# One loop for all rounds in a graph layer: two column groups per step, checks in the middle, a bias product ahead of the last sums

## The chip, the cores and the metric

The kernel runs on one core of a Trainium2 chip. The metric is the device time of one execution in microseconds, the median of several runs. The profile is of one further execution. The span that it shows runs from the first instruction to the last; the time of that execution is a little longer.

## What is computed

Edges carry 128 features each and are sorted by the node `dst` that they point to. Their features are summed per node; node features, sums and one constant row go through a small network, and the result is added to the node features and normalised.

```
agg = segment_sum(edge_attr, dst, num_segments=6250)      # 200000 x 128 -> 6250 x 128
h   = relu(concat([x, agg, u[0]], axis=1) @ W1 + b1)      # 6250 x 128
y   = x + h @ W2 + b2
out = (y - mean(y)) / sqrt(var(y) + 1e-5)                 # per row
```

All is float32. The edge features are 102 MB, by far the largest input; x and the output are 3.2 MB each.

## The kernel before

**Steps and rounds.** 199,680 edges are cut into 65 steps of 3,072 edges (1.5 MB); 320 edges are left as a rest. Steps run from the highest nodes down to node 0; the code counts them with `t`, 0 to 64. Five steps make a round (`lap`, 0 to 12). `dst` follows a square law, so a step near the top spans up to 195 nodes and a step near node 0 only a few. Each round finishes one block of 512 nodes (`BLOCK`), except that the last one leaves only nodes 0 to 127 for the end.

**One step.** VectorE (DVE) makes a one-hot matrix of each run of edges (`hot`, line 580) and one for the rows of partial sums (`row_hot`, line 596). TensorE (PE) does `level1` (line 808): 48 matmuls on 64x32 tiles of its array, each a pair of instructions in the profile, which sum edges into 128 rows of partial sums in PSUM, `rows_ps`. ScalarE (ACT) copies these to SBUF (line 416). PE does `level2` (line 820): two full matmuls that add the rows onto columns, one column per node, in `cols_ps`; DVE adds them to `agg_t` at the step's base column (`add`, line 606), and the next `level2` waits for that addition. The one-hots are made three steps ahead (`AHEAD`).

**Two kinds of rounds.** Rounds 0 to 5 (`sparse_lap`) use 224 columns and put `level2` of step t-1 behind `level1` of step t; `rows_ps` has three buffers. Rounds 6 to 12 (`dense_lap`) use 128 columns and put `level2` of step t right behind `level1` of step t. PE and DVE have a loop for each kind.

**A block of 512 nodes.** x is loaded (ACT's DMA queue), transposed on PE (line 828), copied by ACT (line 436); two products make the hidden layer (line 834 with x, line 843 with `agg_t`); ACT applies relu (line 447); PE multiplies by W2 (line 852); DVE adds (line 618), takes statistics (628, 634, 637) and normalises (643). GpSimd (POOL) adds b2 to x (`bias_add`, line 371) and raises to the power -0.5 (line 380). These pieces stand between the steps of the following round.

**Loads and stores.** SyncE (SP) issues the edge loads into five slots; the load of step t+5 waits for the end of `level1` of step t. The stores of finished blocks stand on SP's queue behind all 65 loads; the last one (line 316) waits for the last normalisation.

```
for t in range(SLOTS, steps):
    sp.wait_ge(level1_done, t - SLOTS + 1)
    load(t)
for i in range(final):
    store(i)
```

**Checks.** The kernel assumes bounds on the nodes that a step reaches. `judge` (DVE, lines 648 to 663) checks them in round 11, PE sums the counts in round 12 (lines 908 to 910) and `make_plan` writes the flag `plan`; were it 0, a slow general path would do all again.

**Filler products.** In the last round PE multiplies `iota` by `ident` into unused columns ahead of steps 62, 63 and 64 (line 901). Nothing reads the result.

## Time and profile before

| what | value |
|---|---|
| median of 3 runs | 281.1 us |
| lowest and highest run | 280.07 and 281.37 us |
| the profiled execution, own time | 281.48 us |
| its span | 279.8 us |
| PE, weight loads (PEld), DVE, ACT, POOL busy | 77%, 60%, 60%, 18%, 15% of the span |
| moved by DMA | 110.06 MB, mean 393 GB/s |
| mean granted clock of TensorE | 0.954 |

The time outside the span is 281.48 - 279.8, some 1.7 us. A busy share is an average over the whole span and says nothing of what a stage waits for. The chain of work that ended last puts 62% on PE and 17% on "issue", time in which the engine waited for nothing that the profile shows; the arrival of a load in SBUF is often such a wait.

### The profile page before, as it was taken

The numbers are of one execution on the slowest core, as the hardware profiler recorded it, in microseconds if no ns is written. First come the engines' busy times: TensorE is split into PE (matmuls) and PEld (weight loads), VectorE is DVE, ScalarE is ACT, GpSimd is POOL, SyncE is SP. The second block draws the span as 40 slices with busy tenths as digits, with TensorE's granted clock in tenths as the row PEclk, the third lists the DMA queues.
The fourth block names the chain that finished last, engine by engine and source line by source line (L and its number), as shares of the span: only waits on it lengthen the run. The fifth ranks groups of instructions, "written<-read, shape, count | busy, mean of one in ns | idle before, by whom it ended". The sixth has DMA issues, their size and how long they took to land.

```text
span 279.8 us, 15302 instructions
## 1 busy us (share of the span) xinstructions
PE 214.5 (77%) x6767; PEld 169.0 (60%) x6767; DVE 167.7 (60%) x425; ACT 51.3 (18%) x100; POOL 40.8 (15%) x49
## 2 busy tenths in 40 slices
PE   0988599986786696696867499898867867767982
PEld 0866487755665575575545378677655655655761
DVE  7932375774665655754854426958565563797552
ACT  0511031311220220221200211322221121120210
POOL 6400020220300400400401100303020030021020
PEclk9986899999999999999997869999999999997998
DMA  7999999999999999999999999999999999999991
GB/s 249 351 387 399 401 399 401 401 400 401 402 399 403 401 400 402 401 401 412 417 411 414 414 401 406 418 417 418 413 418 415 418 416 414 411 418 413 413 396 62
DMA packets 30623, 110.06 MB, mean 393 GB/s; under 512 B 1976, under 2 KB 3150, under 8 KB 30606
## 3 DMA queue, kind: packets, MB, share of 16 engines
q1 hardware_dynamic: 27508, 105.83, 95.3%
q10 hardware_dynamic: 3098, 4.00, 4.1%
q8 instruction: 10, 0.16, 0.2%
q14 instruction: 7, 0.06, 0.1%
HBM read 106.63 MB, written 3.20 MB: 393 GB/s over the span
## 4 chain that ended last, share of the span: by engine, by line
PE 62%; issue 17%; DMA 13%; DVE 5%; POOL 1%; ACT 1%; DVEq 0%; POOLq 0%; ACTq 0%
PE rows_ps L808 33%; PE cols_ps L820 15%; DMA slots<-in_edge_attr 13%; PE hid_ps L852 4%; PE hid_ps L834 3%; PE hid_ps L843 2%; PE hid_ps L828 1%; ACT rows L416 1%; DVE first_of_pair L538 1%; POOL rstd L380 1%; DVE dst_local L548 1%; DVE stats L628 1%; PE rows_ps L967 1%; DVE z L643 0%; DVE agg_t L606 0%
## 5 line engine op out<-in xcount | busy, mean ns | idle before, releaser
L808 PE MATMUL rows_ps<-slots,hot 64*32 64x128 f32 x6240 | 113.3, 285 | 38.4 <-issue 36.4
L808 PEld LDWEIGHTS rows_ps<-slots,hot 64*32 64x32 f32 x6240 | 93.8, 110 | 57.1 <-issue 55.1
L606 DVE TENSOR_TENSOR agg_t<-agg_t,cols_ps 128x128 f32 (+1 forms) x65 | 21.7, 333 | 99.4 <-PE cols_ps L820 99.3
L820 PE MATMUL cols_ps<-row_hot,rows 128*128 128x128 f32 (+1 forms) x260 | 56.2, 340 | 13.3 <-ACT rows L416 5.7
L580 DVE TENSOR_TENSOR hot<-edge_node,iota 128x768 f32<-128x768 f32 x65 | 62.0, 954 | 2.3 <-issue 2.1
L416 ACT ACTIVATE rows<-rows_ps 128x256 f32<-128x256 f32 x65 | 24.9, 383 | 182.6 <-PE rows_ps L808 178.6
L820 PEld LDWEIGHTS cols_ps<-row_hot,rows 128*128 128x128 f32 x260 | 40.4, 196 | 27.2 <-issue 15.2
L380 POOL TENSOR_TENSOR rstd<-var_eps,minus_half 128x4 f32<-128x4 f32 (+1 forms) x13 | 16.6, 1274 | 204.0 <-DVE var_eps L637 204.0
L596 DVE TENSOR_TENSOR row_hot<-row_node,iota 128x256 f32<-128x256 f32 (+1 forms) x65 | 37.6, 578 | 0.0
L371 POOL TENSOR_TENSOR z<-x_rows,b_all 128x512 f32<-128x512 f32 (+1 forms) x13 | 16.5, 1272 | 29.1 <-PE hid_ps L828 29.1
L643 DVE TENSOR_SCALAR z<-z,moments,rstd (+1 forms) x49 | 17.6, 418 | 0.9 <-POOL rstd L380 0.9
L436 ACT ACTIVATE x_t<-hid_ps 128x512 f32<-128x512 f32 (+2 forms) x13 | 13.2, 1018 | 8.0 <-PE hid_ps L828 8.0
L852 PE MATMUL hid_ps<-w_sb,hid 128*128 128x128 f32 x98 | 13.9, 283 | 0.5 <-ACT hid L447 0.5
L834 PE MATMUL hid_ps<-x_t,w1x 128*128 128x512 f32 (+1 forms) x26 | 13.8, 611 | 0.5 <-DVE agg_t L606 0.5
L852 PEld LDWEIGHTS hid_ps<-w_sb,hid 128*128 128x128 f32 x98 | 12.3, 191 | 2.0 <-issue 1.4
L447 ACT ACTIVATE hid<-hid_ps,bias 128x512 f32<-128x512 f32 (+2 forms) x13 | 8.5, 654 | 23.1 <-PE hid_ps L843 20.8
L843 PE MATMUL hid_ps<-agg_t,w1a 128*128 (+1 forms) x24 | 11.7, 570 | 0.5 <-DVE agg_t L606 0.5
L628 DVE BATCH_NORM_STATS2 stats<-z 128x6 f32 (+1 forms) x49 | 10.7, 280 | 0.0
L618 DVE TENSOR_TENSOR z<-z,hid_ps 128x512 f32 (+1 forms) x13 | 8.5, 654 | 1.6 <-PE hid_ps L852 1.6
L828 PE MATMUL hid_ps<-ident,x_rows 128*128 128x128 f32 x49 | 7.7, 277 | 0.8 <-issue 0.2
L843 PEld LDWEIGHTS hid_ps<-agg_t,w1a 128*128 128x128 f32 x24 | 4.5, 189 | 6.0 <-issue 5.2
L828 PEld LDWEIGHTS hid_ps<-ident,x_rows 128*128 128x128 f32 x49 | 5.7, 140 | 2.8 <-issue 2.5
(111 smaller groups left out, 64.8 us busy)
## 6 DMA issues: line engine op xcount, KB each, us to landing
slots<-in_edge_attr SPq DMA_DIRECT2D x65, 1536.0 KB, 17.8
x_rows<-in_x ACTq DMA_DIRECT2D x11, 256.0 KB
out<-z SPq DMA_DIRECT2D x11, 256.0 KB
dst_int<-in_dst SPq DMA_DIRECT2D x1, 384.0 KB, 4.2
dst_int<-in_dst ACTq DMA_DIRECT2D x1, 384.0 KB, 4.6
x_rows<-in_x ACTq DMA_DIRECT2D x1, 192.0 KB
out<-z SPq DMA_DIRECT2D x1, 192.0 KB
rest_slot<-in_edge_attr ACTq DMA_DIRECT2D x1, 160.0 KB, 9.1
```

The lines of the kernel that those rows point to most:

```text
L371: G.tensor_tensor(z[:, bass.ds(i, 1), 0:m, :].rearrange("p o r f -> p (o r) f"), x_rows[:, 0:m, :], b2_all[:, :].unsqueeze(1).broadcast_to ...
L380: G.tensor_tensor(rstd[:, 0:m], var_eps[:, 0:m], minus_half[:, 0:m], ALU.pow).then_inc(rstd_made, 1)
L416: A.activation(rows[i][:, :, :], rows_ps[i][:, :, 0:feats], ACT.Copy).then_inc(rows_copied, 1)
L580: V.tensor_tensor(hot[i][:, :, :], edge_node[:, bass.ds(t, 1), :, :].rearrange("p o c r -> p (o c r)").unsqueeze(2).broadcast_to([P, RUNS, ...
L596: V.tensor_tensor(row_hot[i][:, :, 0:n], row_node[:, bass.ds(t, 1), :].rearrange("p o h -> p (o h)").unsqueeze(2).broadcast_to([P, HALVES, ...
L606: V.tensor_tensor(cols, cols, cols_ps[:, 0:n], ALU.add).then_inc(added, 1)
L643: done = V.tensor_scalar(row(i, r), row(i, r), moments[:, r, 0:1], rstd[:, r:r + 1], ALU.subtract, ALU.mult)
L808: done = T.matmul(rows_ps[i][c * SPAN:(c + 1) * SPAN, h, 0:feats], hot[j][part, c * RUN + r, :], slots[part, j, c, r * feats:(r + 1) * fea ...
L820: done = T.matmul(cols_ps[:, 0:n], rows[i][:, h, :], row_hot[j][:, h, 0:n], start=(h == 0), stop=(h == HALVES - 1))
L834: T.matmul(hid_ps[:, 0:n], w1x[:, :], x_t[:, 0:n], start=True, stop=False)
L843: done = T.matmul(hid_ps[:, 0:n], w1a[:, :], agg_t[:, bass.ds(at, n)], start=False, stop=True)
L852: done = T.matmul(y_ps[:, r, :], hid[:, r * P:(r + 1) * P], w2_sb[:, :], start=True, stop=True)
```

## The change

What it does, part by part:

1. There is one kind of round (`one_lap`) and one loop on PE and DVE (on DVE round 0 stands ahead of it). Each step's `level2` stands behind its own `level1`, with a block's product between them where there is one. `rows_ps` and `rows` have one buffer.
2. A step's columns are two groups of 128, one for each half of its edges. Each group has its own base column. `level2` becomes four matmuls on halves of 64 rows of the array instead of two on all 128; DVE adds two pieces of 128 columns.
3. `judge` runs in round 6 and the plan is made in round 7 (`JUDGE = 6`); the rest of 320 edges is summed and added there too, not ahead of round 1.
4. b2 is no longer added by POOL. PE puts it into its own PSUM bank, `y_bank`, as a product of one row of ones with four copies of b2 (`bias2`, 512 columns, ahead of `level1` of a round's last step), and the products with W2 are added onto it. x is loaded straight into `z`, and ACT copies it to `x_rows` for the transposes.
5. The transposes of x, the hidden layer and the second product have PSUM banks of their own. The product with x stands one round earlier, at the fourth step of its own round.
6. The filler products of the last round are gone.
7. Blocks begin at node 128: the first block is the ragged one, at the top, and only nodes 0 to 127 are left for the end.

```
-COLS = 224
-DENSE_COLS = 128
+COLS = 128
+JUDGE = 6
...
-            def level2(t, j, dense_step):
-                i, n = SETS[j], DENSE_COLS if dense_step else COLS
-                pe.wait_ge(rows_copied, t + 3)
+            def level2(t, j):
+                pe.wait_ge(added, t * GROUPS + 1)
                 pe.wait_ge(row_hot_made, t + 1)
-                pe.wait_ge(added, t + 1)
+                pe.wait_ge(rows_copied, t + 1)
                 for h in range(HALVES):
-                    done = T.matmul(cols_ps[:, 0:n], rows[i][:, h, :], row_hot[j][:, h, 0:n], start=(h == 0), stop=(h == HALVES - 1))
+                    for g in range(GROUPS):
+                        part = slice(g * HALF, (g + 1) * HALF)
+                        done = T.matmul(cols_ps[:, g, 0:COLS], rows[part, h, :], row_hot[j][part, h, :], start=(h == 0), stop=(h == HALVES - 1),
+                                        tile_position=(g * HALF, 0))
                 done.then_inc(level2_done, 1)
...
+            def bias2(seq, m):
+                pe.wait_ge(row_node_made, GROUPS)
+                pe.wait_ge(b2_made, 1)
+                pe.wait_ge(z_made, seq + 1)
+                n = m * feats
+                T.matmul(y_bank[:, 0:n], ones[0:1, :], b2_rows[:, :, :].rearrange("a r f -> a (r f)")[:, 0:n], start=True, stop=False)
...
+            def one_lap(lap):
+                counts(lap)
+                for j in range(LAP):
+                    t = lap * LAP + j
+                    if j == 4:
+                        bias2(lap, ROWS)
+                    level1(t, lap, j)
+                    if j == 0:
+                        with pe.If(lap > 0):
+                            pe.wait_ge(added, t * GROUPS + 1)
+                            product1_agg(lap - 1, start_of(lap - 1))
+                        with pe.If(lap == JUDGE + 1):
+                            rest_and_bounds()
+                    elif j == 1:
+                        with pe.If(lap > 0):
+                            product2(lap - 1, lap - 1)
+                    elif j == 2:
+                        turn_x(lap)
+                    elif j == 3:
+                        product1_x(lap, BLOCK)
+                    level2(t, j)
...
-            def dense_lap(lap):
...
-                        with pe.If(lap > final - 1):
-                            if j == 4:
-                                product1_x(final, final)
-                                pe.wait_ge(plan_made, 1)
-                            pe.wait_ge(rows_copied, laps * LAP - LAP + j + 1)
-                            T.matmul(rows_ps[SETS[j]][:, 0, feats:512], ident[:, :], iota[:, feats:512], start=True, stop=True)
...
+            def add(t, at):
+                dve.wait_ge(level2_done, t + 1)
+                for g in range(GROUPS):
+                    dve.wait_ge(added, t * GROUPS + (g + 1))
+                    cols = agg_t[:, bass.ds(at[g], COLS)]
+                    V.tensor_tensor(cols, cols, cols_ps[:, g, 0:COLS], ALU.add).then_inc(added, 1)
...
-            def bias_add(seq, i):
-                m = rows_of(i)
-                pool.wait_ge(x_turned, seq + 1)
-                G.tensor_tensor(z[:, bass.ds(i, 1), 0:m, :].rearrange("p o r f -> p (o r) f"), x_rows[:, 0:m, :],
-                                b2_all[:, :].unsqueeze(1).broadcast_to([P, m, feats]), ALU.add).then_inc(z_ready, 1)
```

The first place where the prediction looks at the order is PE's queue at the end of a round, from the `level2` of step j = 3 to the end of the loop. Before (the second loop; the piece between the two L894 runs in the last round alone):

```order
L820 MATMUL cols_ps<-row_hot,rows 128x128 x2
L894 COMPARE_AND_BRANCH
L834 MATMUL hid_ps<-x_t,w1x 128x128
L901 MATMUL rows_ps<-iota,ident 128x384
L894 UNCONDITIONAL_BRANCH
L808 MATMUL rows_ps<-slots,hot 32x128 x48
L820 MATMUL cols_ps<-row_hot,rows 128x128 x2
L972 REGISTER_ALU
L972 COMPARE_AND_BRANCH
L843 MATMUL hid_ps<-agg_t,w1a 128x128
L852 MATMUL hid_ps<-w_sb,hid 128x128
```

And the same place in the changed kernel, from the `level1` of step j = 3 (L773) on; L786 is `level2` and L813 `bias2`:

```order
L773 MATMUL rows_ps<-slots,hot 32x128 x48
L801 MATMUL hid_ps<-x_t,w1x 128x512
L786 MATMUL cols_ps<-row_hot,rows 128x128 x4
L813 MATMUL y_bank<-b_rows,ones 128x512
L773 MATMUL rows_ps<-slots,hot 32x128 x48
L786 MATMUL cols_ps<-row_hot,rows 128x128 x4
L894 REGISTER_ALU
L894 COMPARE_AND_BRANCH
L805 MATMUL hid_ps<-agg_t,w1a 128x128
L818 MATMUL y_bank<-w_sb,hid 128x128
```

The filler and the branch around it are gone; a product of 512 columns with x now stands ahead of `level2` of the fourth step, and the b2 product ahead of `level1` of the fifth, in every round.

The second place is DVE's queue at a round's second step (j = 1). Before, in the second loop, the branch L704 is taken in round 11:

```order
L606 TENSOR_TENSOR agg_t<-agg_t,cols_ps 128x128
L618 ISA
L618 TENSOR_TENSOR z<-z,hid_ps 128x512
L704 COMPARE_AND_BRANCH
L648 TENSOR_REDUCE high<-dst_int 128x4
L649 TENSOR_REDUCE lowest<-dst_int 128x4
```

In the changed kernel, where L579 is the addition, L590 the residual and the branch L676 is taken in round 6:

```order
L579 TENSOR_TENSOR agg_t<-agg_t,cols_ps 128x128
L579 ISA
L579 TENSOR_TENSOR agg_t<-agg_t,cols_ps 128x128
L590 ISA
L590 TENSOR_TENSOR z<-z,y_bank 128x512
L676 COMPARE_AND_BRANCH
L653 CAST rest_node<-rest_int 64x5
L654 TENSOR_TENSOR rest_hot<-rest_node,iota 64x160
L620 TENSOR_REDUCE high<-dst_int 128x4
L621 TENSOR_REDUCE lowest<-dst_int 128x4
```

A step has two additions, one behind the other, and the checks with the rest's one-hots stand five rounds earlier.

## Rows read from the trace of the kernel before

**Rows 1.** Page, part 2: the span in 40 equal slices of 7 us (clock, DMA busy share, GB/s).
```profile
PEclk9986899999999999999997869999999999997998
DMA  7999999999999999999999999999999999999991
GB/s 249 351 387 399 401 399 401 401 400 401 402 399 403 401 400 402 401 401 412 417 411 414 414 401 406 418 417 418 413 418 415 418 416 414 411 418 413 413 396 62
```

**Rows 2.** Loads of line 304 issued in four short windows: issue time, time until landed.
```profile
L304 SPq DMA_DIRECT2D slots<-in_edge_attr x1: 368/368/368, 169.2 to 169.2; - x1
...
DMA to landing us min/median/max: 7.9/7.9/7.9
...
L304 SPq DMA_DIRECT2D slots<-in_edge_attr x1: 368/368/368, 231.4 to 231.4; - x1
...
DMA to landing us min/median/max: 17.9/17.9/17.9
...
L304 SPq DMA_DIRECT2D slots<-in_edge_attr x1: 368/368/368, 247.3 to 247.3; - x1
...
DMA to landing us min/median/max: 17.3/17.3/17.3
...
L304 SPq DMA_DIRECT2D slots<-in_edge_attr x1: 368/368/368, 251.1 to 251.1; - x1
...
DMA to landing us min/median/max: 17.2/17.2/17.2
```

**Rows 3.** Timeline of round 11: start, us, engine, line [idle before it].
```profile
241.96 1.75 DVE L648 TENSOR_REDUCE high<-dst_int 128x4 f32<-128x1536 int32 x1
...
247.25 0.96 DVE L580 TENSOR_TENSOR hot<-edge_node,iota 128x768 f32<-128x768 f32 x1
...
248.47 0.28 DVE L606 TENSOR_TENSOR agg_t<-agg_t,cols_ps 128x128 f32 x1
...
249.51 1.59 PE L808 MATMUL rows_ps<-slots,hot 64*32 64x128 f32 x96
...
251.29 1.33 POOL L371 TENSOR_TENSOR z<-x_rows,b_all 128x512 f32<-128x512 f32 x1
251.42 1.48 DVE L596 TENSOR_TENSOR row_hot<-row_node,iota 128x256 f32<-128x256 f32 x1
...
252.82 0.28 DVE L606 TENSOR_TENSOR agg_t<-agg_t,cols_ps 128x128 f32 x1
...
253.25 0.68 PE L820 MATMUL cols_ps<-row_hot,rows 128*128 128x128 f32 x4 [2.15 <-DVE agg_t L606]
```

**Rows 4.** Chain that ended last, five of its pieces: start, us, what.
```profile
59.94 0.86 PE hid_ps L834 x2
...
235.24 1.05 PE hid_ps L834 x2
...
240.54 0.45 PE cols_ps L820 x4
...
254.22 2.97 PE rows_ps L808 x96
...
263.30 0.65 PE rows_ps L901 x2
```

**Rows 5.** Timeline of the last step: start, us, engine, line [idle before it].
```profile
270.85 1.59 PE L808 MATMUL rows_ps<-slots,hot 64*32 64x128 f32 x96
...
272.93 0.71 PE L820 MATMUL cols_ps<-row_hot,rows 128*128 128x128 f32 x4 [0.49 <-ACT rows L416]
...
273.78 0.29 DVE L606 TENSOR_TENSOR agg_t<-agg_t,cols_ps 128x128 f32 x1 [2.28 <-PE cols_ps L820]
...
274.12 0.49 PE L843 MATMUL hid_ps<-agg_t,w1a 128*128 128x128 f32 x2 [0.48 <-DVE agg_t L606]
...
277.74 0.37 SPq L316 DMA_DIRECT2D out<-z  x1
```

**Rows 6.** Busy time of PE, PEld, DVE, ACT, POOL, then clock, DMA, GB/s, 200 to 220.
```profile
200.00:220.00 20.00, 14.73 (x549) 11.58 (x532) 11.50 (x31) 3.70 (x7) 2.29 (x2) 1.00 1.02 417
```

459 lines of the change are left out of this document (184 added, 275 removed).

## The prediction

> **What bounds the kernel now.** I first read the page's slices [rows 1]. Behind the first three, the DMA line stands at 9 tenths up to the last slice and the rate lies near 400 GB/s, later near 415. So the stream of edge loads is never empty, and in the middle its bytes set the pace, not an engine. What the reader has to look for then is only how far the work trails behind the last load.
>
> Each load's issue and its time to landing [rows 2] say so step by step. The load of step 59 was issued at 231.4 us and landed 17.9 us later, at 249.3; `level1` of step 59 begins at 249.51 [rows 3]. TensorE (PE) waited for data there and began 0.2 us after they came: it rides on the stream. The load of step 63 lands at 247.3 + 17.3 = 264.6, that of step 64, the last, at 251.1 + 17.2 = 268.3. But `level1` of step 64 begins at 270.85 [rows 5]. Riding on the stream it would begin at 268.3 + 0.2 = 268.5. In the last round the kernel is 2.35 us late against its own data, and that is all that a change can win ahead of the last step. From 270.85 to the end of the span, 279.8, a serial tail of 8.95 us follows: `level1`, copy, `level2`, addition at 273.78, product at 274.12, and the rest up to the store at 277.74 [rows 5].
>
> Where does the lateness come from? The timeline of round 11 shows it [rows 3]. `judge` holds VectorE (DVE) from 241.96 to 247.25, 5.3 us, and the addition behind it ends near 248.75. DVE is still behind when it makes `row_hot` at 251.42, and this one takes 1.48 us, beside POOL's addition of b2 at 251.29, which takes 1.33. The addition comes at 252.82, PE's `level2` of step 59 at 253.25 after 2.15 us of idleness, and `level1` of step 60 at 254.22, about 0.9 after it could have. This idle stretch also cost the clock: the same 96 instructions took 2.97 us [rows 4] where step 64's take 1.59 [rows 5], about the ratio of the two levels, 1.2 and 2.4 GHz; the page's clock line dips there too, to 7 [rows 1]. From then on PE has to catch up, and it cannot do so quickly, since three filler products of 0.65 us each [rows 4] stand in its way.
>
> **The change part by part.**
>
> *Checks moved to rounds 6 and 7, b2 off POOL.* Both causes of the late step 60 leave round 11. The same 5.3 us of DVE now fall near step 31, together with two small operations for the rest. There they cost nothing, because loads are queued: the shallowest moment before, behind the start of the second loop, had a load land 7.9 us after its issue [rows 2], two loads deep, and the stream never stopped (417, 411, 414 GB/s in those slices [rows 1]). On the stream's heels the depth is 17.9 us; less some 5.3, about 12 remain. If this cover were gone, the price would be up to 5.3 us, but it needs a stall some 10 us longer. The start of the second loop goes too, with its stalls, and for the same reason wins nothing.
>
> *The last round.* Nothing now keeps PE off the stream up to step 63. It begins at 264.6 + 0.2 = 264.8 and ends 1.59 later, at 266.4. Then, in the order of the new queue: the product with x, 512 columns, 1.05 us behind a `level1` [rows 4]; `level2`; the b2 product; `level1` of step 64.
> - `level2`: before, 0.45 us in its shortest form [rows 4]. Now it is eight instructions on half the rows each. If the two halves run side by side it stays 0.45; one behind the other it is 0.9. 
> - b2: 512 columns and one row of weights, no such row before. The nearest is the product with x, 0.86 us [rows 4], in the same form of two instructions. Below lies 0 (if it fits into the wait for data), above 1.05, the same product behind another tiling.
>
> The sum: 266.4 + 1.05 + 0.45 + 0.86 + 0.4 = 269.15, against 270.85. With the lower values PE would be ready at 268.75 or before, and the stream at 268.5 decides almost alone; with a serial `level2` it is 269.6. So `level1` of step 64 begins 1.7 us earlier (1.25 to 2.35).
>
> The Trainium skill speaks against this part: the page "TensorEngine Tiling (Array Packing)", section "Key Properties", says that changing the tiling mode drains TensorE. The trace agrees in direction, by the 0.2 us between the two rows of the product with x; by the page alone, without a figure, every one of the new changes would cost a drain, and by the rows without it the sum would be 268.75. The page "TensorE: Matmul & The Clock Gate", section "The mechanism", has matmuls in different row groups overlap; that is the 0.45 rather than the 0.9.
>
> *The tail.* Two additions now stand where one stood, the second waiting for the first: 0.29 us [rows 5] and some 0.04 for the wait, +0.33. `level2` of step 64 took 0.71 [rows 5] with its weights late; eight instructions take 0 to 0.45 more, and I take 0. The rest of the tail has the same instructions on 128 columns as before; the b2 addition of POOL was not on it.
>
> *At no price.* The single `rows_ps`: `level2` of rounds 0 to 5 now waits for ACT's copy within its step, some 0.5 us [rows 5], as in rounds 6 to 12 before. PE is busy 14.73 of 20 us between 200 and 220 at full clock [rows 6], DVE 11.50; a round's extra work is 0.86 for b2 on PE, five additions of 0.29 on DVE and one copy on ACT. All of it hides behind a step's load, which comes every 3.7 to 4 us. If that cover were gone, each round would pay some 0.9. The loads of weights and x are issued in another order ahead of the first step; the first steps run before the stream's depth is used up, so a later first step by 1 us is hidden as well.
>
> *Sum.* 1.7 won, 0.33 lost: 1.37 us, call it 1.4. The profiled execution took 281.48, so 280.1 for one like it. It is the slowest of those known, 0.4 above the median of 281.1; against the median the forecast is 279.7.
>
> **The rivals.** What this kernel's measurement can tell from no change is about 0.5%, 1.4 us: below 279.7 counts as faster, above 282.5 as slower.
> - *The forecast* (chance 0.45), between 279.1 and 280.3, half of it on each side of 279.7.
> - *PE rides on the stream to the end* (0.14): the b2 product fits into the wait and tiling costs nothing. `level1` of step 64 at 268.5: 2.35 - 0.33 = 2.0, so 279.1. For it: the 0.86 beside 1.05 may be the weights' order alone. Against it: 1.59 + 1.05 + 0.45 + 0.86 is 3.95, and step 64's data come 3.7 behind step 63's.
> - *The stream itself ends earlier* (0.06), since the first loads meet other neighbours on the queues and less code is fetched. The slices at the start are at 249 and 351 GB/s [rows 1]; a tenth of the missing 150 x 7 and 50 x 7 us is worth some 0.4 us. With the forecast's 1.4 it gives 279.3 or less, down to 278.5. Against it: the same bytes in the same queues.
> - *The halves of `level2` run one behind the other* (0.15). It costs 0.45 before step 64 and 0.45 in the tail: 1.37 - 0.9 = 0.5 won, 280.6.
> - *The last round begins late anyway* (0.08): DVE in its third step has two additions (0.6 us), the statistics (1.7: from 248.75 to 251.42 less one `hot` of 0.96) and the one-hots (1.2: from 247.25 to 248.47) [rows 3], 3.5 us of the 3.7 that a step has. If this is late again without `judge`, step 60 is late by as much as before; only the three fillers (1.95) go, while the b2 product and the wider product with x (1.7) come: 281.1 + 0.1 and up, with the second addition 281.2.
> - *Slower: the clock falls in the last round* (0.12). The fillers kept PE busy where now it waits for data. If the clock is at 1.2 GHz from step 63 on, its `level1` takes 2.97, the three products twice their 2.36, and step 64 begins at 264.8 + 2.97 + 4.7 = 272.5 with 1.4 more for itself and about 1 for `level2` and the products of the tail: 1.65 + 2.4 + 0.33 = 4.4 lost, 285.5. From step 64 on alone it is 1.37 - 2.4, 282.1; it counts as slower from somewhat ahead of step 64 on. Against it: rounds 8 to 10 ran without fillers, with about 1 us of idleness in a step, and from 200 to 220 the clock is 1.00 [rows 6]. It fell only after more than 2 us of it [rows 3].
>
> **How the numbers follow.** The predicted time is the forecast's, 279.7. Faster: half of the forecast (0.22), the ride (0.14), the early stream (0.06), 0.42. Same: the other half, the serial halves and the late round, 0.46. Slower: 0.12. The range must leave out no more than 2 in 10. It reaches from 278.5 (the early stream) to 281.8, past the late round and the scatter of the runs (280.07 to 281.37) around it, and leaves out the clock's fall and little else. The forecast's own range is 279.0 to 280.3.
>
> **What the profile after will show.** The last edge load lands at 268.3, give or take 0.5. `level1` of step 60 begins some 0.2 us behind its data, not 1. `level1` of step 64 begins at 269.15; its distance to step 63's start is 4.35, of which b2 is 0.86. Two additions stand between the last `level2` and the last product, 0.33 more. The landing times stay near 18 us, dip behind step 31 by about 5 and come back. The clock line shows no dip in slice 36 or 37. I am wrong if the last load lands at another time, if the clock falls in round 12, if `level2` takes over 0.8 us where nothing holds it, or if something at the start costs more than the queued loads cover.

## The result, and the profile after

| what | before | after |
|---|---|---|
| median | 280.37 us (18 runs, 278.80 to 281.60) | 281.96 us (18 runs, 279.76 to 283.18) |
| ratio after / before | | 1.0061, 95% interval 1.004 to 1.0081 |
| the profiled execution, own time and span | 281.48 and 279.8 us | 281.76 and 280.0 us |
| mean granted clock | 0.954 | 0.973 |

The changed kernel is 0.6% slower, just outside the forecast's range of 278.5 to 281.8. The forecast was 279.7 us, 1.4 below the first median of before; the three runs known then (281.1) lay high, 18 runs give 280.37. The two profiled executions differ by 0.2 us of span only, because the one of before is among its slowest and the one of after is near its own median. So the traces show what is won and lost where, and only many runs show how often. All ratios, here and below, are taken over the executions in the fast state, so they need not be the quotient of two medians.

The page of after, its slices of 7 us (clock, DMA, GB/s), against [rows 1]:

```profile
PEclk9999859999999999999999999999999999999996
DMA  7999999999999999999999999999999999999991
GB/s 258 365 360 399 400 400 326 402 401 402 400 401 402 401 402 400 402 401 411 417 416 414 420 419 415 415 418 417 419 415 416 416 417 419 416 413 417 415 400 66
```

The seventh slice, 42 to 49 us, moves 326 GB/s where its neighbours move 400. The stream of loads ran dry there, which costs (400 - 326) / 400 of 7 us, 1.3 us. The DMA line still shows a 9: it hides a hole of this size, the GB/s line doesn't. In [rows 1] the hole stands in slices 24 and 25, 401 and 406 GB/s; the prediction quoted 417, 411 and 414, the slices ahead of them.

The loads around the hole, and the last two, each as issue time and time until landed:

```profile
L315 SPq DMA_DIRECT2D slots<-in_edge_attr x2: 367/368/368, 35.2 to 43.2; - x2
...
DMA to landing us min/median/max: 7.6/8.9/10.3
```

```profile
L313 SPq DMA_DIRECT2D slots<-in_edge_attr x2: 367/367/367, 247.9 to 252.1; - x2
...
DMA to landing us min/median/max: 16.8/17.0/17.3
```

The load of step 8 lands at 35.2 + 10.3 = 45.5, that of step 9 at 43.2 + 7.6 = 50.8: 5.3 us apart instead of 3.9. This load took 7.6 us; in e_delay, below, one that was issued after the load ahead of it had landed took 6.5. So, as an estimate from these two, a load must be issued 2.6 to 3.7 us (6.5 or 7.6, less 3.9) before the one ahead of it lands, here by 41.8 to 42.9, and it was issued at 43.2. It waits for the end of `level1` of step 4. In the kernel before, the same load was issued at 36.2, some 6 us ahead of that limit. The last load lands at 252.1 + 16.8 = 268.9, against 268.3 in [rows 2].

The GB/s line does not show all that is lost. The load of step 16 lands at 80.0, 5.1 us behind that of step 15, but fourteen of its 16 queues are done by 78.4. By then two queues trail, and they do so to the end: of the last load, fourteen end by 266.7 and the two others at 268.0 and 268.9. Why they stay behind is open.

The last rounds, timeline of after (start, us, engine, line, idle before it), against [rows 3] and [rows 5]:

```profile
253.98 1.58 PE L773 MATMUL rows_ps<-slots,hot 64*32 64x128 f32 x96 [0.60 <-DMA slots<-in_edge_attr]
...
266.79 1.13 PE L801 MATMUL hid_ps<-x_t,w1x 128*128 128x512 f32 x2
...
267.84 0.71 PE L786 MATMUL cols_ps<-row_hot,rows 64*128 64x128 f32 x8
...
268.49 1.12 PE L813 MATMUL y_bank<-b_rows,ones 1*128 1x512 f32 x2
...
269.54 1.59 PE L773 MATMUL rows_ps<-slots,hot 64*32 64x128 f32 x96
...
272.56 0.71 DVE L579 TENSOR_TENSOR agg_t<-agg_t,cols_ps 128x128 f32 x2 [2.11 <-PE cols_ps L786]
...
273.32 0.49 PE L805 MATMUL hid_ps<-agg_t,w1a 128*128 128x128 f32 x2 [0.89 <-DVE agg_t L579]
...
276.48 0.35 DVE L615 TENSOR_SCALAR z<-z,moments,rstd 128x128 f32<-128x128 f32 x1 [0.66 <-POOL rstd L378]
```

Step 60 (the first line) is on time: it waits for its data, begins 0.1 us behind them and takes 1.58 us, with a granted clock of 1.00. Step 64 begins 0.64 us behind its data (269.54 - 268.9), against 2.5. From its start to the end of the last normalisation it is 7.3 us, against 6.9; from there to the end of the span 3.2, against 2.0. The account, in us of span: the last landing +0.6, the lateness behind it -1.9, the additions +0.4, the end +1.15; together +0.25, where the spans say 0.2.

Where does the late `level1` of step 4 come from? PE in round 0, first before, then after (an idle time put down to "issue" is one in which PE waited for nothing that the profile shows):

```profile
12.45 2.81 PE L808 MATMUL rows_ps<-slots,hot 64*32 64x128 f32 x96
15.20 0.38 PE L930 MATMUL rows_ps<-u_col,w1u 64*128 64x1 f32 x2
...
17.37 1.12 PE L808 MATMUL rows_ps<-slots,hot 64*32 64x128 f32 x61
...
32.69 0.90 PE L820 MATMUL cols_ps<-row_hot,rows 128*128 128x224 f32 x2 [2.83 <-issue]
33.53 2.56 PE L808 MATMUL rows_ps<-slots,hot 64*32 64x128 f32 x96
```

```profile
13.79 2.81 PE L773 MATMUL rows_ps<-slots,hot 64*32 64x128 f32 x96
17.30 1.23 PE L786 MATMUL cols_ps<-row_hot,rows 64*128 64x128 f32 x8 [0.70 <-ACT rows L408]
...
23.09 1.23 PE L786 MATMUL cols_ps<-row_hot,rows 64*128 64x128 f32 x8 [0.60 <-ACT rows L408]
...
27.67 0.65 PE L795 MATMUL turn_bank<-ident,x_rows 128*128 128x128 f32 x4
...
34.48 0.67 PE L773 MATMUL rows_ps<-slots,hot 64*32 64x128 f32 x11 [3.99 <-issue]
35.08 2.08 PE L801 MATMUL hid_ps<-x_t,w1x 128*128 128x512 f32 x2
...
38.24 2.07 PE L813 MATMUL y_bank<-b_rows,ones 1*128 1x512 f32 x2
40.24 2.81 PE L773 MATMUL rows_ps<-slots,hot 64*32 64x128 f32 x96
```

Step 4 begins at 40.24 instead of 33.53, 6.7 us later. That splits into: step 0 starts later, 1.3; ACT's copy waited for in the open twice, 1.3; transposes, product with x and b2's product, which now stand ahead of step 4, 4.8, the two products at TensorE's lower clock (2.08, against 1.13 at the end of the kernel; the granted clock is 0.50 from 34 to 42 us); longer `level1`, 1.2; more of the "issue" stalls (5.25 in all, against 4.93), 0.3; less the bias and rest products that stood between steps 0 and 1, 2.2. The granted clock does not explain all of the longer `level1`: step 1 takes 3.4 us without its stall, about twice the full clock's 1.59, and the column reads 1.00 there. The stalls lie beside transfers of code: the trace's instruction queue brings 16 KB at 32.1 us, in the stall of 3.99. Each of the three stalls in either kernel ends 1.3 to 1.5 us after a transfer of 16 KB does. That the transfer causes the stall is argued from this, not tested.

### The profile page after: what moved, and what is told of

It is laid out like the page before. It is cut to its first block, busy times and chain, and to the rows that moved or that the text cites. A ratio compares the mean times of both kernels' runs of the same rounds, so it can differ in the third digit from the quotient of the medians.

```text
span 280.0 us, 15858 instructions
## 1 busy us (share of the span) xinstructions
PE 224.8 (80%) x7044; PEld 163.5 (58%) x7044; DVE 167.2 (60%) x487; ACT 58.6 (21%) x111; POOL 21.7 (8%) x39
## 4 chain that ended last, share of the span: by engine, by line
DMA 46%; PE 40%; issue 7%; DVE 5%; ACT 1%; POOLq 0%; DVEq 0%; POOL 0%; ACTq 0%
DMA slots<-in_edge_attr 44%; PE rows_ps L773 21%; PE cols_ps L786 7%; PE hid_ps L801 2%; PE y_bank L813 2%; PE hid_ps L805 2%; PE y_bank L818 2%; DMA dst_int<-in_dst 2%; PE turn_bank L795 1%; ACT rows L408 1%; DVE dst_local L534 1%; DVE lowest L621 1%; DVE high L620 1%; DVE agg_t L579 1%; DVE z L615 0%
## 5 line engine op out<-in xcount | busy, mean ns | idle before, releaser
L773 PE MATMUL rows_ps<-slots,hot 64*32 64x128 f32 x6240 | 109.2, 280 | 29.3 <-issue 22.7
L773 PEld LDWEIGHTS rows_ps<-slots,hot 64*32 64x32 f32 x6240 | 91.1, 108 | 48.9 <-issue 47.1
L579 DVE TENSOR_TENSOR agg_t<-agg_t,cols_ps 128x128 f32 x130 | 37.4, 288 | 98.4 <-PE cols_ps L786 89.2
L786 PEld LDWEIGHTS cols_ps<-row_hot,rows 64*128 64x128 f32 x520 | 36.1, 192 | 38.2 <-issue 32.3
L786 PE MATMUL cols_ps<-row_hot,rows 64*128 64x128 f32 x520 | 48.0, 303 | 10.9 <-ACT rows L408 6.6
L569 DVE TENSOR_TENSOR row_hot<-row_node,iota 128x256 f32<-128x256 f32 x65 | 27.1, 417 | 0.0
L801 PE MATMUL hid_ps<-x_t,w1x 128*128 128x512 f32 x26 | 15.6, 683 | 0.0
L813 PE MATMUL y_bank<-b_rows,ones 1*128 1x512 f32 x26 | 15.5, 678 | 0.0
L818 PE MATMUL y_bank<-w_sb,hid 128*128 128x128 f32 x98 | 14.4, 289 | 0.5 <-ACT hid L434 0.5
L423 ACT ACTIVATE x_t<-turn_bank 128x512 f32<-128x512 f32 x12 | 13.2, 1104 | 2.2 <-PE turn_bank L795 2.2
L818 PEld LDWEIGHTS y_bank<-w_sb,hid 128*128 128x128 f32 x98 | 11.9, 191 | 3.0 <-issue 2.4
L434 ACT ACTIVATE hid<-hid_ps,bias 128x512 f32<-128x512 f32 (+1 forms) x13 | 8.6, 663 | 11.6 <-PE hid_ps L805 11.6
L590 DVE TENSOR_TENSOR z<-z,y_bank 128x512 f32 (+1 forms) x13 | 8.4, 650 | 1.5 <-PE y_bank L818 1.5
```

Of the source, the lines that this page charges most:

```text
L569: V.tensor_tensor(row_hot[i][:, :, :], row_node[:, bass.ds(t, 1), :].rearrange("p o h -> p (o h)").unsqueeze(2).broadcast_to([P, HALVES, C ...
L579: V.tensor_tensor(cols, cols, cols_ps[:, g, 0:COLS], ALU.add).then_inc(added, 1)
L773: done = T.matmul(rows_ps[c * SPAN:(c + 1) * SPAN, h, 0:feats], hot[j][part, c * RUN + r, :], slots[part, j, c, r * feats:(r + 1) * feats] ...
L786: done = T.matmul(cols_ps[:, g, 0:COLS], rows[part, h, :], row_hot[j][part, h, :], start=(h == 0), stop=(h == HALVES - 1), tile_position=( ...
L801: T.matmul(hid_ps[:, 0:n], w1x[:, :], x_t[:, 0:n], start=True, stop=False)
L813: T.matmul(y_bank[:, 0:n], ones[0:1, :], b2_rows[:, :, :].rearrange("a r f -> a (r f)")[:, 0:n], start=True, stop=False)
```

## The experiments

Each run is compared with runs of the kernel before on the same chip, between them; the ratio is to those.

| run | median us | ratio, 95% interval |
|---|---|---|
| c_before, kernel before | 279.78 | 0.9971 (0.9945 to 0.9997) |
| c_after, changed kernel | 283.0 | 1.0099 (1.0061 to 1.0137) |
| e_round0 | 282.17 | 1.0045 (1.0012 to 1.0078) |
| e_nogeneral | 283.72 | 1.0121 (1.0088 to 1.0154) |
| e_delay | 284.37 | 1.0129 (1.0088 to 1.0169) |
| e_b_delay | 280.88 | 1.0015 (0.999 to 1.0041) |
| e_judge11 | 286.09 | 1.0171 (1.0129 to 1.0213) |
| e_b_early | 278.95 | 0.9951 (0.9929 to 0.9974) |
| e_next | 283.2 | 1.0103 (1.007 to 1.0136) |
| e_next_split | 284.12 | 1.0144 (1.011 to 1.0178) |
| e_b_early9 | 278.83 | 0.9949 (0.9926 to 0.9971) |
| e_next_nogen | 281.5 | 1.0044 (1.0019 to 1.007) |
| e_b_serial | 280.05 | 0.999 (0.9962 to 1.0018) |
| e_cover | 282.3 | 1.0037 (1.0007 to 1.0067) |
| c_after_again, changed kernel | 282.28 | 1.007 (1.004 to 1.0099) |
| e_port | 281.3 | 1.0036 (1.001 to 1.0062) |
| e_port_round0 | 280.21 | 0.9991 (0.9968 to 1.0014) |
| e_b_port | 278.74 | 0.9947 (0.9926 to 0.9968) |

The kernel before differs from itself by 0.3% (c_before), so a difference of 0.3% between two runs proves nothing alone.

The second run of the changed kernel, c_after, was expected to show the hole again. Its profiled execution, at 279.9 us its fastest, has none: `level1` of step 4 ends at 41.1 us instead of 43.1, steps 8 and 9 land 3.9 us apart, and the last load lands at 266.8. c_after_again, 283.1 us, has wide gaps at steps 10 and 12 and its last load at 269.6. So the hole comes in some executions and not in others, and the time goes with it.

### The start: is it the margin of step 4?

The theory: the loss is the hole at step 9, and it appears when `level1` of step 4 ends too late. e_delay and e_b_delay put four products more (`ident` with `iota`, 512 columns, read by nobody) into step 3 of round 0 of the changed kernel and of the kernel before.

```
elif j == 3:
    with pe.If(lap < 1):
        for _ in range(4):
            T.matmul(hid_ps[:, 0:BLOCK], ident[:, :], iota[:, :], start=True, stop=True)
```

> The changed kernel with four products of 512 columns more on TensorE's queue in round 0 (ident times iota, results unused), ahead of the product with x: 3.4 us at the full clock, 8 us at the low one. Theory A (the edge stream runs empty in round 0 because level1 of step 4 ends too late): whatever is added there beyond the cover goes into the time one for one; the gap ahead of the landing of step 9's load grows to about 8 us or more, and the time rises by 3 us or more over the changed kernel, ratio to the kernel before about 1.02. Theory B (only the tail matters): no change, 1.006 to 1.010.

> The kernel before with the same four products in its round 0. There the load of step 9 was issued with 13.3 us to go, that of the changed kernel with 7.6 us, and about 7.5 us is where the stream begins to show a gap; so before has some 5.7 us of cover. Theory A: at the full clock (3.4 us) nothing changes, ratio 1.000; at the low clock (8 us) some 2 us are lost. The gap ahead of step 9's landing tells which. Theory B: 1.000.

`level1` of step 4 in e_delay and in e_b_delay, and between them the loads of steps 8 and 9 in e_delay:

```profile
44.81 1.59 PE L773 MATMUL rows_ps<-slots,hot 64*32 64x128 f32 x96
...
L315 SPq DMA_DIRECT2D slots<-in_edge_attr x2: 368/368/368, 35.9 to 46.5; - x2
...
DMA to landing us min/median/max: 6.5/8.1/9.7
...
37.06 1.59 PE L808 MATMUL rows_ps<-slots,hot 64*32 64x128 f32 x96
```

In e_delay it ends at 46.4 us, and steps 8 and 9 land 7.3 us apart (45.6 and 52.9). In e_b_delay it ends at 38.7 us and there is no hole there. With the four products the changed kernel goes from 1.0061 and 1.0099 to 1.0129, less than the 1.02 that was expected and with an interval that overlaps c_after's, and the kernel before to 1.0015, nothing that can be told. The traces carry the argument more than the medians do: the kernel before has the margin, the changed one has used it up.

e_round0 puts the two early products of round 0 behind step 4:

```
level1(t, lap, j)
if j == 4:
    with pe.If(lap < 1):
        product1_x(lap, BLOCK)
        bias2(lap, ROWS)
```

> The changed kernel, but in round 0 alone the product with x and the b2 product stand behind level1 of step 4 instead of ahead of it (one branch more on TensorE's queue at each). Theory A: level1 of step 4, which ended at 43.2 us with both products at the low clock ahead of it (2.1 us each), ends about 4 us sooner, the stream does not run empty, all later loads land 1.0 to 1.4 us sooner, and the ratio to the kernel before falls from 1.006 to about 1.001. Theory B: no change, 1.006.

```profile
36.97 2.81 PE L773 MATMUL rows_ps<-slots,hot 64*32 64x128 f32 x96
39.71 1.34 PE L801 MATMUL hid_ps<-x_t,w1x 128*128 128x512 f32 x2
40.99 1.12 PE L813 MATMUL y_bank<-b_rows,ones 1*128 1x512 f32 x2
```

Step 4 begins 3.3 us earlier than in the changed kernel, steps 8 and 9 land 3.9 us apart, and the last load lands at 266.8. The time hardly follows: 1.001 was expected and 1.0045 came, with an interval that overlaps both c_after's (1.0099) and that of the first comparison (1.0061). The trace is of an execution of 280.8 us, and five of the twelve took 282.6 to 283.3. Both products are cheaper there, 2.46 us against 4.15; the granted clock is 0.95 from 40 to 42 us.

e_next goes further and sets both products, in every round, into the next round's steps 0 and 1, beside the products that they belong with. It was to be the better kernel.

> The changed kernel with the two early products set later: the product with x of a round and b2's product both stand in the next round, in front of the products that they belong with (x's behind level1 of its first step, b2's behind level1 of its second), so round 0 holds neither, and the last block's two stand behind level2 of step 64, ahead of the wait for DVE's last addition. Theory (the start is lost by the two products at TensorE's low clock in round 0, the end by nothing in the products): level1 of step 4 ends by about 39.5 us (the changed kernel 40.8 and 42.6), loads of tiles 8 and 9 land 3.9 us apart (5.24 in the changed kernel's first profile), the last tile lands at about 266.8, level1 of step 64 starts within 0.3 us of it (0.6 in the changed kernel, since b2's product no longer stands ahead of it), the span is 277.5 to 278.3 and the ratio to the kernel before 0.990 to 0.997. Rival (the start's loss comes from code fetches and TensorE's clock and not from these products, since the other order of round 0 gave only 1.0045): the gap at tile 9 stays in some executions and the ratio is 1.002 or more.

It failed: 1.0103. PE in e_next (timeline), and the window 30 to 50 us of e_next and of c_after (busy time of PE, PEld, DVE, ACT, POOL, then the granted clock, DMA, GB/s):

```profile
39.38 2.51 PE L773 MATMUL rows_ps<-slots,hot 64*32 64x128 f32 x96
42.55 0.68 PE L786 MATMUL cols_ps<-row_hot,rows 64*128 64x128 f32 x7 [0.66 <-ACT rows L408]
...
45.57 2.82 PE L773 MATMUL rows_ps<-slots,hot 64*32 64x128 f32 x96 [0.71 <-issue]
48.31 1.13 PE L801 MATMUL hid_ps<-x_t,w1x 128*128 128x512 f32 x2
```

```profile
30.00:50.00 20.00, 14.07 (x346) 10.72 (x328) 5.43 (x13) 2.61 (x5) 0.00 (x0) 0.74 0.96 363
```

```profile
30.00:50.00 20.00, 16.11 (x438) 11.07 (x434) 7.21 (x17) 2.74 (x6) 0.00 (x0) 0.87 1.03 400
```

The products left round 0 and came back in round 1, where PE is still behind. Steps 4 and 5 ran at the lower level of 1.2 GHz (2.5 and 2.8 us instead of 1.6), and over this window PE was granted 0.74 instead of c_after's 0.87. That the missing products caused this is not shown: over the same window the other traces of the changed kernel have 0.74 (after) and 0.66 (c_after_again). The hole moved to steps 10 to 12. This execution also had the accident described below, but the one of e_next_split had not: step 4 ends at 40.1 there, 3 us earlier than in the changed kernel, and the hole is 6.5 us, at step 12. What counts is not only when step 4 ends but how long PE stays behind the loads.

e_cover tries the clock from the other side: short products in steps 0, 1 and 4 of round 0, where PE waits for the copy.

```
if j in (0, 1, 4):
    with pe.If(lap < 1):
        T.matmul(few_ps[:, P:2 * P], ident[:, :], iota[:, 0:P], start=True, stop=True)
```

> The changed kernel with three short products (128 columns, result used by nobody) in round 0 alone, in steps 0, 1 and 4, between level1 and level2, where TensorE waits 0.6 to 0.7 us for ACT's copy; the output is the same. Theory that the idle stretches keep TensorE's clock low in the first 45 us: the clock is full again by level1 of step 4 (1.3 to 1.6 us instead of 2.4), which ends 1 us earlier than in the changed kernel (40.8 to 42.6) or at least not later, ratio 1.002 to 1.006. Rival (the clock falls in the code-fetch stalls of 2.5 to 4 us, which no cover shortens, and the copies' waits matter only as time): the three products cost 0 to 0.2 us each beyond the wait, level1 of step 4 ends 0 to 0.5 later, clock as in the changed kernel, ratio 1.006 to 1.012.

Its ratio is 1.0037, below c_after's and c_after_again's, with an interval that overlaps both. Its profiled execution, one of its three slowest, has `level1` of step 4 at the lower clock all the same, 43.3 to 46.1. Whether the cover helps is not settled.

e_b_serial gives the kernel before the open copy alone: rounds 0 to 5 in the order of its rounds 6 to 12.

```
-                    if j:
-                        level2(t - 1, j - 1, False)
...
+                    level2(t, j, False)
```

> The kernel before with its rounds 0 to 5 in the order of its rounds 6 to 12: level2 of a step directly behind that step's level1 (and behind the round's product, if there is one), instead of behind the next step's level1, so TensorE waits for ACT's copy in most steps. Two loops, 224 columns, one addition, fillers and late bounds stay. Theory (the open copy is the largest part of the changed kernel's later start): TensorE waits 0.5 to 0.7 us for ACT's copy in each of the first steps, level1 of step 4 ends at 37.5 to 39.5 us (before 34.5 to 35.8, changed kernel 40.8 to 42.6), which is still ahead of the 41 to 42 at which the stream breaks; so the last tile lands as before, at 268.3, and the ratio is 0.999 to 1.004, with single executions above. Rival (as forecast: the copy is hidden by other work, the products and TensorE's clock make the late start): level1 of step 4 ends by 36.5, ratio within 0.002 of 1.

The ratio is 0.999: an open copy in every step of six rounds does not slow the kernel before by anything that can be told. Its profiled execution shows waits of 0.47 to 0.63 us for the copy, and something else:

```profile
8.20 3.24 DVE L552 TENSOR_SCALAR base_diag<-ident,base 128x64 f32<-128x64 f32 x1
```

`base_diag` takes 0.47 us in the first trace of before. DVE reached the next operation 2.8 us later, PE began step 0 at 15.27 instead of 12.45, ended step 4 at 42.4, and step 9 landed 5.8 us behind step 8. Without the 2.8, if the rest had stayed as it was, step 4 would have ended at 39.6, about where the theory had it. With them, one accident at 8 us, this form of the kernel before had the changed kernel's hole too, and still took 279.92 us, near its median.

### The start: GpSimd's clearing and one operation of VectorE

The same in e_cover, DVE and POOL side by side:

```profile
8.67 3.43 POOL L369 MEMSET agg_t<- 128x512 f32 x8 [2.39 <-DVE dst_local L534]
8.77 3.41 DVE L539 TENSOR_SCALAR base_diag<-ident,base 128x128 f32<-128x128 f32 x1
```

POOL clears `agg_t` in eight instructions without a gap, and `base_diag` ends with the last of them. Of the 17 profiled executions with this order, of either kernel, `base_diag` took about 0.5 us in ten, 0.93 to 0.96 in three, and 3.2 to 3.4 in four. It is the same code each time within a kernel; now and then DVE does not get in between. The Trainium skill, page "GPSIMD Engine Reference", section "Specifications", lists POOL's SBUF interfaces as shared with VectorE, in contention with some forms of its instructions. The rows agree as far as the two operations end together here, and they add that the loss differs from one execution to the next; whether `base_diag` is of such a form no run here shows. The cure is one line, POOL waits for `base_diag`:

```
-            pool.wait_ge(local_made, SHARE)
+            pool.wait_ge(base_made, 1)
             for a, b in pieces_of_agg[blocks // 2:]:
```

> The changed kernel with GpSimd's second batch of clearing agg_t (3.4 us) set behind VectorE's base_diag instead of behind dst_local, ahead of it. Theory (GpSimd's clearing holds the memory port that base_diag needs, in some executions for all 3.4 us, and the changed kernel, whose level1 of step 4 ends at 40.8 to 42.6 without it, then breaks its stream): base_diag takes 0.3 to 0.5 us, level1 of step 0 starts at 13.3 to 14.3, the timed executions lose their upper part, median 0.8 to 2 us below the changed kernel's in this call, ratio 0.999 to 1.004. Rival (it was scatter of no weight, or the clearing now shuts out a later copy of VectorE, row_node's): median within 0.5 us of the changed kernel's, ratio 1.006 to 1.01, another operation of VectorE between 9 and 14 us takes 3 us.

> The changed kernel unchanged, beside e_port: ratio 1.004 to 1.012 as in its first comparisons (1.0061 and 1.0099), with executions spread over 4 us or more. If its profiled execution has base_diag at over 3 us, its stream breaks once by 2 us or more at tile 8 to 12 and the last tile lands at 270 or later; with base_diag at 0.5 to 1.0 it lands at 266.8 to 269.

> Run e_port with the order of run e_round0 as well: in round 0 the product with x and b2's product behind level1 of step 4. Theory (start margin adds up: 3 us from the products in round 0, up to 3 from the collision): level1 of step 4 ends at 36.5 to 39.5 in every execution, no gap over 4.7 us in rounds 1 and 2, last tile lands at 266.8, ratio 0.993 to 0.999, below e_port by 0.5 us or more. Rival (what the products give back is taken by TensorE's low clock, as in e_next): same as e_port within 0.5 us.

> The run e_b_early9 (kernel before, judging in round 9, plan in round 10, no fillers) with GpSimd's clearing behind base_diag. Theory: this kernel has 6 us of margin ahead of the point at which its stream breaks in the start, so the collision of 2.8 us cost it nothing there; ratio as e_b_early9 within 0.2%, 0.993 to 0.997, scatter alike. Rival (the start counts here as well): 1 us or more below e_b_early9, ratio 0.990 or less.

`base_diag` now takes 0.28 us:

```profile
8.78 0.28 DVE L539 TENSOR_SCALAR base_diag<-ident,base 128x128 f32<-128x128 f32 x1
```

The changed kernel wins 1.0 us by it, measured side by side (282.28 to 281.3; the intervals overlap), and its slowest execution of twelve falls from 285.0 to 283.07. The cure alone does not close the hole. The profiled execution of e_port is its slowest, and the load of step 10 there reads:

```profile
L315 SPq DMA_DIRECT2D slots<-in_edge_attr x1: 368/368/368, 48.0 to 48.0; - x1
...
DMA to landing us min/median/max: 8.2/8.2/8.2
```

It lands at 56.2, 6.4 us behind step 9, though `base_diag` took 0.28. c_after_again, with `base_diag` at 0.5, has gaps of 5.5 and 5.2 us at steps 10 and 12 and its last load at 269.6, later than the 266.8 to 269 that were expected. So the hole does not need the collision.

With the order of e_round0 as well as the cure the time is 280.21, and all twelve executions lie between 279.83 and 280.92, where the changed kernel spreads over 281.05 to 285.0. The two ratios, 0.9991 and 1.007, have intervals that are clear of each other: earlier steps at the start give back some 2 us. How that divides between the order and the cure is open, since each alone gave a difference within the noise. In the kernel before, which has the margin, the cure moves nothing (e_b_port is e_b_early9, described below, with the cure: 0.9949 to 0.9947). That is what the theory of the margin says. The last load of e_port_round0:

```profile
L313 SPq DMA_DIRECT2D slots<-in_edge_attr x1: 367/367/367, 249.6 to 249.6; - x1
...
DMA to landing us min/median/max: 16.8/16.8/16.8
```

It lands at 249.6 + 16.8 = 266.4, 1.9 us ahead of before's 268.3: no hole in the start, and none in the middle; from step 3 on no two landings are over 4.7 us apart.

### The middle: one loop or two

> The kernel of the run e_next with TensorE's one loop written as two, rounds 0 to 5 and rounds 6 to 12, with the same body. Theory (the second loop's first pass costs code fetches, which put off level1 by so much that the stream of loads breaks once): a gap of 5 us or more between two landings near tile 42 (3.9 everywhere in the run e_next), after it one of the 16 queues lands about 1.6 us behind the others, the last tile lands 1.4 to 1.6 us later than in the run e_next, ratio 0.005 above that run's. Rival (as forecast: the buffers' slack of over 3 us takes the stall, a second loop costs nothing): same landings, same ratio within 0.002.

e_next with PE's loop written as two (rounds 0 to 5, rounds 6 to 12) has a gap of 5.0 us at step 42 and is 0.9 us slower than e_next, 1.0144 against 1.0103, with intervals that overlap. The later landing that was expected did not come: its last load lands at 270.6, that of e_next, which had the collision, at 271.8. In the kernel before two loads near that place read:

```profile
L304 SPq DMA_DIRECT2D slots<-in_edge_attr x2: 368/368/368, 169.2 to 172.2; - x2
...
DMA to landing us min/median/max: 7.9/9.1/10.3
```

Step 41 lands at 169.2 + 7.9 = 177.1 [rows 2], step 42 at 172.2 + 10.3 = 182.5: 5.4 us apart. From then on one of the 16 queues ends each load some 1.6 us behind the fifteenth, up to step 64 (266.7 and 268.3). So it is one queue that falls behind there more than a stream that runs dry: the rate loses only some 0.3 us of bytes, by 401 and 406 GB/s beside 414. Traces without a hole there, c_after and e_port_round0, have their last load at 266.8 and 266.4. The instruction queue brings 16 KB five times from 138 to 180 us in the kernel before, and nothing from 130 to 185 us in the changed kernel. So the second loop seems to cost some 1.5 us. This is argued from the landings and not shown by a pair of runs, and it does not happen each time: e_b_serial has two loops and no gap over 4.7 us in the middle. Why one queue stays behind is open.

### The last rounds: checks and b2

e_judge11 puts the changed kernel's `judge` back into round 11 (`JUDGE = 11`), and with it the work for the rest of 320 edges; e_b_early puts the kernel before's into rounds 7 and 8 and drops the fillers; e_b_early9 uses rounds 9 and 10.

> The changed kernel with the checks back in round 11 (JUDGE = 11), the rest's sum then in round 12. If the checks were what made step 60 late before (the prediction's step), level1 of step 60 begins about 1 us behind its data again, the clock falls for it, and the time rises by 1 to 2 us over the changed kernel, ratio 1.012. Rival: POOL's b2 addition, which is gone, was the larger part of the lateness; then step 60 is on time, and the time rises by under 0.5 us, by the rest's products at most.

> The kernel before with two of the change's parts alone: the checks in rounds 7 and 8 instead of 11 and 12, and no filler products. By the account of the last round, level1 of step 64 begins within 0.3 us of its data instead of 2.5 us behind; tail and start stay as before; 2.0 to 2.3 us are won, ratio 0.992. Rival: without the fillers the clock falls in the last round, and the ratio is 1.00 or more. Rival: the checks beside the start of the second loop, which already stalls TensorE, break the stream there, 1 us or more lost, ratio 0.996 to 1.00.

> The kernel before with its bounds judged in round 9 and the plan in round 10 instead of the last two, without the filler products; round 7 in the run e_b_early stood beside the start of the second loop, whose stream broke twice (5.01 and 5.79 us at tiles 41 and 44; once in the kernel before). Theory: with the judging in round 9 only one break stands (at tile 42 or 43), the last tile lands at 268.3 (270.2 in e_b_early), level1 of step 64 starts within 0.2 us of it, span 277.5 to 278, ratio 0.990 to 0.994. Rival (the lateness of the judging hits whichever round has it and the stream breaks there): landings of round 9 or 10 are 5 us apart, the last tile lands at 270, ratio 0.995 as e_b_early.

```profile
251.29 0.72 PE L786 MATMUL cols_ps<-row_hot,rows 64*128 64x128 f32 x8 [1.97 <-DVE agg_t L579]
251.94 1.68 PE L813 MATMUL y_bank<-b_rows,ones 1*128 1x512 f32 x2
253.55 2.81 PE L773 MATMUL rows_ps<-slots,hot 64*32 64x128 f32 x96
```

With the checks late, PE of the changed kernel waits 1.97 us for DVE's addition in step 58, the granted clock falls from 1.00 to 0.50 (from 254 us on), and step 64 begins 5.9 us behind its data (1.0171). The profiled execution is the slowest of its six, so 5.9 is an upper case. With the checks early and the fillers gone, and nothing else changed, the kernel before becomes the fastest of all here, 0.995: step 64 begins 0.1 us behind its data in both traces. The two together are thus worth 0.5%, some 1.4 us, where 0.992 had been expected; their shares were not separated. POOL still adds b2 there, and step 60 is on time in both traces (252.87 and 252.96 in e_b_early9), so taking b2 off POOL was not needed for it. Round 9 instead of 7 saves the second hole beside the loop's start in the trace (the last load lands at 268.1 instead of 270.2), yet the medians are alike. The trace of e_b_early is of its slowest execution, 281.21 us, and may not be typical; the forecast of a further gain was wrong, or the gain is below what can be told.

### The end: code behind the last branch

e_nogeneral leaves out the general path (and SP's read of the flag); the result is the same as long as the bounds hold. e_next_nogen does it to e_next.

> The changed kernel without the slow general path at the end of each engine's program; it never runs with these inputs, so it is only the code that the engines jump over. Theory B (the end fetches code): the time from the last normalisation to the end falls from 3.2 us to 2.0 or less, ratio 1.002. Theory A alone: the end stays at 3.2 us and the ratio at 1.006. If both hold, this run gives 1.002 and the one on round 0 gives 1.001.

> The kernel of the run e_next without the general path (the code that all engines jump over when the bounds hold, and SyncE's read of the plan; the output is the same here as long as the bounds hold). Theory (the 1.2 us from the last normalise to the end come from code that DVE fetches from beyond the jump while the last store is landing): from the last normalise's end to the end of the span 1.95 us as in the run e_nogeneral, against 3.2 to 3.5 in e_next, so 1.2 to 1.5 us less span at the same landings; ratio 0.986 to 0.992. Rival (the end's time is the store's own, 2 us or more, whatever the code): 3.2 us stay. The gap at tile 9 was 6.48 us in e_nogeneral, against 5.24 in the changed kernel; if the missing code moves the code fetches of round 0, it may come back here, and the last tile then lands at over 268.

SP's wait for the last store, 64 KB, in the changed kernel and then in e_nogeneral (us in total, times, longest):

```profile
SPq L104 <- DMA out<-z: 2.0, 1, 2.0
```

```profile
SPq L104 <- DMA out<-z: 1.2, 1, 1.2
```

From the last normalisation to the end it is 3.2 us in the changed kernel and 1.95 in e_nogeneral; 3.2 and 2.1 in e_next and e_next_nogen. In the changed kernel's trace two transfers of 8 KB on the instruction queue start at 277.7 and 277.9, when DVE has done its last operation and the store is under way; the kernel before and e_nogeneral have one, and need 2.0 us. e_next_nogen is 1.7 us faster than e_next, measured side by side (281.5 against 283.2). e_nogeneral itself was not faster, 1.0121, where 1.002 was expected. Its profiled execution had `base_diag` at 3.41 us and a hole of 6.5 us in the start, but that execution was the fastest of its six (282.06), so why the others are slower still is open. The shorter end is shown by the traces and supported by the second pair; that it is DVE's code behind the jump is argued, since the edit takes the general path from every engine. The path alone is not enough for the loss: the kernel before has it too, and ends in 2.0 us.

## Why the prediction was wrong

*The stream bounds the middle.* Right, and the reason why PE's and DVE's extra work in the middle cost nothing.

*Checks early, b2 off POOL.* Right for the checks: step 60 waits for its data, e_b_early wins by it with the fillers gone, and e_judge11 loses by undoing it. Taking b2 off POOL was named as the second cause, and the runs do not bear that out: e_b_early9 leaves it on POOL and step 60 is on time.

*The last round, 269.15.* Right in the mechanism and near in size (269.54). From step 63's start to step 64's it was to be 4.35 us; it is 4.27, at 265.27 and 269.54. Start to start, the product with x holds PE for 1.05, `level2` for 0.65 and b2 for 1.05, where the forecast had 1.05, 0.45, 0.86 and 0.4 for the tilings: the halves of `level2` run side by side, and, if the excess over 0.45 and 0.86 is that, the changes of tiling cost some 0.2 each. That the total fits is in part luck: `level2` is 0.2 above its term and b2 0.2 above its own, and together they take up the 0.4 that was set down for the tilings.

*The tail, +0.33.* The additions cost 0.43. Not foreseen is the end: +1.15 us in the first pair of traces, +1.5 in e_port. The prediction said that the rest of the tail has the same instructions. It has, but the last store takes 2.0 us to land instead of 1.2, beside one more transfer of code.

*The start, "At no price".* This is the step that failed. It allowed a first step later by 1 us, and took the depth of the queued loads, read at 169 us and at 231 us [rows 2], for the depth at 40 us. In the start there is no such depth: the first steps begin 4.7 us and more apart (13.8, 18.5, 24.3, 29.0, 40.2; stalls and the lower clock), slower than the data come. Step 4 ended 5 to 8.5 us later, over the traces of both kernels as they are, and the margin before was some 6. What goes beyond it is lost in the stream: 1.3 us at step 9 in the changed kernel's first trace, 3.4 in e_delay's. The prediction named this itself as a sign of being wrong ("something at the start costs more than the queued loads cover"), but no rival had it and no chance was set on it. The same paragraph costs the product of b2 and the copy for one round in the middle; in round 0 they stand in a row with the product with x, at the low clock. None of these alone is shown to be decisive (e_b_serial, e_round0, e_next), nor is the collision (e_port). Taking the products out of the way and curing the collision together brings the median from 282.28 to 280.21.

*The second loop "wins nothing".* Probably wrong as well. The hole of before at step 42 was in the loads but not in the slices that were quoted. One loop seems worth some 1.5 us; e_port_round0's last load, 1.9 us ahead of before's, agrees. It also means that the 2.35 us of lateness were not, as the prediction had it, all that could be won ahead of the last step.

*The clock in the last round.* The rival did not come; without fillers the clock line shows 9 up to the last slice but one.

*The sum.* Forecast, against before: -1.7 ahead of step 64, +0.33 behind it. Shown, in a clean execution (e_port_round0 against the first trace of before, spans 278.0 and 279.8): -1.9 by the landing, -1.9 by the lateness, +0.6 by additions and products of the tail, +1.5 at the end, together -1.7. In the traces of the changed kernel with wide gaps (after, c_after_again) the last load lands 2.5 and 3.3 us later than that. The best version is neither kernel: the kernel before with early checks and no fillers, 278.83, or 278.74 with the cure, which cannot be told apart.

## What to carry to other kernels

A stream that bounds a kernel has a margin, and it differs from place to place: read it, in each stage, as the time between a load's issue and the landing of the load ahead of it, and do not carry the depth of the middle over to the start. A change that folds two loops into one adds to the first round work that used to be skipped; list what stands ahead of the last load that fills a slot for the second time. When single executions of one kernel differ by 3 us, compare the first microseconds of several traces before explaining the medians.

## What the runs showed of the hardware

- DVE's `base_diag`, 0.25 to 0.29 us when POOL waits for it, took 0.5, 0.95 or 3.2 to 3.4 us beside eight clearing instructions of POOL; the changed kernel alone showed 0.5 and 0.96.
- In the first pass through the loop PE stood still for 5 us in the open in its first steps, in both kernels (4.93 and 5.25), with a 16 KB transfer of code before the end of each: all six stalls end 1.3 to 1.5 us after such a transfer does. With a second loop such transfers come again, from 138 to 180 us. That they cause the stalls is not tested.
- With the general path left out, the time from the last normalisation to the end fell by 1.1 us (e_next to e_next_nogen) and 1.25 us (the changed kernel to e_nogeneral); the last store landed in 1.4 and 1.2 us instead of 2.0.
- One of 16 queues can fall 1.6 us behind the others and stay behind for some 85 us (the kernel before, steps 42 to 64).
- A load of 1.5 MB issued after the one ahead had landed took 6.5 us (e_delay, e_cover, e_nogeneral); in the full stream they land 3.9 us apart.
